# Macaron block: the mixer's three normalizations written by ScalarE instead of VectorE

## What is computed

```python
def _layernorm(x, axis=-1, eps=1e-05):
    m = jnp.mean(x, axis=axis, keepdims=True)
    v = jnp.var(x, axis=axis, keepdims=True)
    return (x - m) / jnp.sqrt(v + eps)

def _rmsnorm(x, w):
    v = jnp.mean(x * x, axis=-1, keepdims=True)
    return x * jax.lax.rsqrt(v + EPS) * w

# inside the mixer step, x is the layernorm of the stream
h = x + _mixer(_rmsnorm(x, norm1_w), in_proj_w, conv_w, conv_b, A_log, dt_bias, D, out_proj_w)
hn = _rmsnorm(h, norm2_w)
ffn = jax.nn.silu(hn @ gate_w.T) * (hn @ up_w.T) @ down_w.T
return h + ffn

# the whole
x = x + 0.5 * _L0_ffn_ref(_layernorm(x), ...)
x = x + _L0_attn_ref(_layernorm(x), ...)
x = x + 0.5 * _L0_ffn_ref(_layernorm(x), ...)
```

## Time and profile before

| what | us |
|---|---|
| median of 3 runs | 972.69 |
| lowest and highest of them | 969.92, 974.05 |
| the profiled execution | 979.37 |
| its span, first to last instruction | 977.6 |
| busy in the span: TensorE, its weight load | 718.4, 473.1 |
| busy: VectorE, ScalarE, GpSimd | 594.9, 364.3, 406.6 |
| VectorE on L1120, L959, L1195 in 300 to 700 us | 8.8, 7.8 (28 of 32), 7.0 |

### The profile page before, as it was taken

How to read it: one execution, slowest core, us unless ns; L and a number is a source line. 1 busy time by engine, 2 the same in 40 slices (tenths; PEclk the granted TensorE clock), 3 DMA queues, 4 the chain that set the end, 5 groups by cost and what they waited for, 6 DMA issues and landing times. The chain is left out here.

```text
span 977.6 us, 12866 instructions
## 1 busy us (share of the span) xinstructions
PE 718.4 (73%) x3584; PEld 473.1 (48%) x3584; DVE 594.9 (61%) x1898; ACT 364.3 (37%) x600; POOL 406.6 (42%) x540
## 2 busy tenths in 40 slices
PE   5777178887729689899998898686787537888860
PEld 3455157776503445353536354343454326777650
DVE  5744244454366888897887888873673333445427
ACT  2112033443308656656656565520111103344320
POOL 3755745554522333232332323210276562555550
PEclk9977579999959799999999999887788667999975
DMA  7311222222150000000000000000011122222208
GB/s 224 124 39 41 72 64 69 76 69 61 40 172 1 0 1 1 0 1 1 1 0 2 0 1 1 0 1 1 0 42 44 38 66 74 73 66 75 69 27 258
DMA packets 55892, 46.30 MB, mean 47 GB/s; under 512 B 8840, under 2 KB 51437, under 8 KB 55824
## 3 DMA queue, kind: packets, MB, share of 16 engines
q1 hardware_dynamic: 47120, 28.55, 10.7%
q0 software_dynamic: 8704, 16.93, 5.2%
HBM read 25.31 MB, written 21.19 MB: 48 GB/s over the span
## 5 line engine op out<-in xcount | busy, mean ns | idle before, releaser
L627 POOL DMA_INDIRECT ys<-arena,dest x144 | 140.8, 978 | 143.6 <-DVE arena L1444 89.3
L617 POOL DMA_INDIRECT xs<-rows,pos x128 | 124.3, 971 | 76.8 <-DVE pos L1364 39.0
L1820 PE MATMUL ps_go<-w_down_e,arena 128*128 x576 | 79.0, 281 | 8.7 <-DVE arena L1444 7.9
L1820 PEld LDWEIGHTS ps_go<-w_down_e,arena 128*128 128x128 f32 x576 | 71.5, 195 | 11.3 <-issue 11.3
L1434 DVE TENSOR_TENSOR hid<-silu_a,ps_b 128x512 f32<-128x512 f32 x36 | 24.7, 686 | 59.1 <-issue 36.2
L1783 PE MATMUL ps_tr<-ident,arena 128*128 128x128 f32 x144 | 29.9, 285 | 40.9 <-DMA arena<-xs 40.7
L1809 PE MATMUL ps_go<-ident,hid 128*128 128x128 f32 x288 | 44.8, 279 | 19.0 <-ACT arena L896 17.1
L1444 DVE COPY arena<-ps_go 128x256 f32<-128x256 f32 x72 | 30.5, 424 | 45.3 <-remote 28.2
L879 ACT ACTIVATE xt_hi<-ps_tr 128x256 fp32r<-128x256 f32 x72 | 27.6, 383 | 81.6 <-PE ps_tr L1783 73.3
L896 ACT ACTIVATE arena<-ps_go 128x512 f32<-128x512 f32 x72 | 43.0, 597 | 38.6 <-remote 31.2
L1537 PE MATMUL ps_a<-arena,w_tap 128*32 128x512 f32 (+1 forms) x120 | 56.0, 611 | 0.0
(11 more groups left out here) (275 smaller groups left out, 1843.7 us busy)
## 6 DMA issues: line engine op xcount, KB each, us to landing
arena<-xs SPq DMA_DIRECT2D x144, 65.0 KB
rows<-ys SPq DMA_DIRECT2D x8, 512.0 KB, 4.2
arena<-ys SPq DMA_DIRECT2D x8, 512.0 KB, 7.7
ys<-arena,dest POOLq DMA_INDIRECT x144
x<-in_L_attn_x SPq DMA_DIRECT2D x8, 256.0 KB, 6.4
arena<-in_L_ffn_ew SPq DMA_DIRECT2D x4, 512.0 KB, 7.1
xs<-rows,pos POOLq DMA_INDIRECT x128
out<-x SPq DMA_DIRECT2D x8, 256.0 KB, 3.6
```

Source lines behind the costliest of these rows:

```text
L617: pool.indirect_dma_start(xs, bass.IndirectOffsetOnAxis(pos[:, n, k * TT + t:k * TT + t + 1], 0), rows[:, n * TT + t, :], None).then_inc(s ...
L627: pool.indirect_dma_start(ys, bass.IndirectOffsetOnAxis(dest[:, i:i + 1], 0), y_out[:, p % YRING, j, :], None, bounds_check=2 * TOK - 1, o ...
L1820: r = pe.matmul(ps_k[:, j * P:(j + 1) * P], hid_t[:, p % 2, at:at + P], w_down_e[:, bass.ds(which[2 * p + j], 1), k, :].rearrange("p a d - ...
```

## The change

All three normalizations move to ScalarE, as activations with a factor column as scale and, for the first two, an offset column as bias: (x - mean) * r becomes x * r + (-mean * r). GpSimd makes the offsets, three small instructions more a block, and `azr` becomes two buffers deep, as is `offset`. The offsets stand before `arstd_ready` is raised. Two new waits in `pool_norms` guard the buffers against readers of two blocks earlier. In ScalarE's body `z_norm` stands ahead of `zt_copy`, `h_norm` ahead of `hnt_copy`, and `h_start` last. `enter` on VectorE loses its normalization between two `combine` steps.

```diff
-        azr = sb("azr", [P, TT])
+        azr = sb("azr", [P, 2, TT])
+        offset = sb("offset", [P, 2, 2, TT])
...
         def pool_norms(pool, b, q):
...
             pool.wait_ge(amv_ready, n + 1)
+            after(pool, zn_ready, n - 1)
+            after(pool, hb_ready, n - 1)
...
-            pool.tensor_tensor(azr[:, :], arstd[:, q, :], asmall[:, 0, :], ALU.mult).then_inc(arstd_ready, 1)
+            step(pool.tensor_tensor(azr[:, q, :], arstd[:, q, :], asmall[:, 0, :], ALU.mult))
+            step(pool.tensor_scalar(asmall[:, 1, :], amv[:, q, :, 0], -1.0, None, ALU.mult))
+            pool.tensor_tensor(offset[:, q, 0, :], asmall[:, 1, :], azr[:, q, :], ALU.mult)
+            pool.tensor_tensor(offset[:, q, 1, :], asmall[:, 1, :], arstd[:, q, :], ALU.mult).then_inc(arstd_ready, 1)
...
         def act_mixer(act):
+            def z_norm(b, q):
+                n = SQ * b + q
+                act.wait_ge(arstd_ready, n + 1)
+                after(act, zt_ps_ready, n)
+                for t in range(TT):
+                    r = act.activation(zn[:, t, :], x_tile(b, q, t), ACT.Identity, bias=offset[:, q, 0, t:t + 1],
+                                       scale=azr[:, q, t:t + 1])
+                r.then_inc(zn_ready, 1)
+            def h_start(b, q):
+                n = SQ * b + q
+                act.wait_ge(arstd_ready, n + 1)
+                after(act, hnt_ps_ready, n)
+                for t in range(TT):
+                    r = act.activation(hb[:, t, :], x_tile(b, q, t), ACT.Identity, bias=offset[:, q, 1, t:t + 1],
+                                       scale=arstd[:, q, t:t + 1])
+                r.then_inc(hb_ready, 1)
+            def h_norm(b, q):
+                n = SQ * b + q
+                act.wait_ge(hr_ready, n + 1)
+                for t in range(TT):
+                    r = act.activation(hb[:, t, :], hb[:, t, :], ACT.Copy, scale=hsm[:, 2, t:t + 1])
+                r.then_inc(hn_ready, 1)
...
                 if then:
+                    z_norm(*then)
                     zt_copy(*then)
...
                 if now:
+                    h_norm(*now)
                     hnt_copy(*now)
...
                     tm_copy(*next, 0)
+                    h_start(*next)
             def enter(n):
+                z_norm(*n)
                 zt_copy(*n)
...
-        def dve_mixer_norm(dve, b, q):
...
-            def h_start(b, q):
...
-            def h_norm(b, q):
...
             def enter(n):
...
                 combine(1)
-                combine(2)
-                dve_mixer_norm(dve, *n)
-                for m in range(3, NB):
+                for m in range(2, NB):
                     combine(m)
```

More of the change, by code:

```diff
@@ L486, in pool_norms @@
             n = SQ * b + q
-            own = Steps(pool, own_pool_pre, 6, n)
+            own = Steps(pool, own_pool_pre, 8, n)
             def step(instruction):
@@ L671, in act_mixer, with x_tile @@
             owns = [None]
+            def x_tile(b, q, t):
+                return x[:, (b * SQ + q) * TT + t, :]
+            def z_norm(b, q):
[20 more added lines that the diff above has]
+                r.then_inc(hn_ready, 1)
             def step(instruction):
@@ L1225, in body @@
                     outputs(*now, 0)
-                if then:
-                    dve_mixer_norm(dve, *then)
                 if now:
@@ L1252, in body @@
                     phase_sums(*next)
-                if now:
-                    h_norm(*now)
                 if next:
@@ L1275, in body @@
                     c_relative(*next)
-                    h_start(*next)
             def enter(n):
```

## The result

Run in turn, the changed kernel took 976.69 us (median of 20 runs, 970.43 to 983.66), the kernel before 971.01 (20 runs, 963.93 to 976.64). The ratio is 1.0068, with a 95% interval of 1.0046 to 1.009: the change made the kernel slower by 5.7 us, or 0.7%. The forecast was +7.9.

The account below looks back on a forecast made before the run. VectorE is busiest, but ScalarE, GpSimd and TensorE arrive just ahead, so relief is waited away. Entry 3.7, first pass 0.7, slow-clock passes 2 x 0.5, last two 1.4 and 0.4, clock 0.7: +7.9 on 972.7, 980.5 us; range 972 to 987.

Parts of the forecast that it names:

- What one group costs: Moved norms on ScalarE: 0.49 us per two-column instruction, 1.66 a group of four; `h_norm` 0.40 each, 1.3 a group.
- Rival A: ScalarE's second column is free and the groups are short: 4.6 us slower in all, 977 us; chance 0.22.
- GpSimd's part: The offset steps on GpSimd ahead of the norms add 0.76 us; the new buffer waits add nothing.
- A pass: Mixer pass with three blocks in flight: about 0 change for the fast kind, 0.5 us longer where TensorE was already later.
- (1): Pass head: `h_start` on ScalarE pushes `dt_parts` by 1.56 us, 0.62 absorbed by a gap, so `dt_sum` comes 0.94 later.
- (4): Pass end: `h_norm` adds 0.43 us, `hn_ready` is 0.54 later, and VectorE waits at `ffn_hidden(0)`, losing the 1.5 saved.
- Rival C: VectorE sets the pass, so passes give 1.5 us back: -3.5 us, or 957 us with the heads; chance 0.08.
- The entry: Mixer start, without cover: block 0 costs 1.3 us and block 1 2.4 us more, 3.7 in all, all kept.
- First full pass: Pass from 331 to 378 us: a ScalarE gap hides `h_start`; GpSimd's 0.76 and `h_norm` make it 0.7 us longer.
- the clock: TensorE's wait before `h_norm`'s transposes grows from 2.2 to about 2.6 us; half a pass more at lower clock, 0.7 us.
- rival B: TensorE's clock falls in all passes after the longer wait, three more at 1.34 us each: 984 us; chance 0.18.
- Pass without `then`: Pass 8, with no block to normalize at its head: `h_start` adds 0.94 us and `h_norm` 0.43, 1.4 in all.

Follow-up runs that it names:

- first pair: One profiled execution each of the kernel before and the changed kernel, all three norms on ScalarE; the mixer parts sum to 411.6 and 415.1 us.
- second pair: One more profiled execution each of the kernel before and the changed kernel, in a later session; the mixer took 408.0 and 417.6 us.
- second session: The unmodified changed kernel run again beside the kernel before; ratio 1.0093 (1.006 to 1.0126), +8.3 us.
- b_moved: Changed kernel with ScalarE's `h_start` moved ahead of `ffn_copy`, into the gap at the end of a pass; ratio to the kernel before 1.0045.
- a_znorm: Kernel before with only `z_norm` moved to ScalarE, plus GpSimd's offsets; ratio 1.0124, +12.0 us.
- a_pool: Kernel before with GpSimd making the offsets and holding `arstd_ready` for them, all three norms still on VectorE; ratio 1.0046, +3.7 us.

## Why the prediction was right, by its own steps

**What one group costs: right.** 478 to 482 ns against 0.49, groups of 1.63 to 1.65 us against 1.66, 387 ns against 0.40 for one column. From 298 ns without a column the first adds 89 and the second 91 to 95, where the forecast had 108 for one and 0.49 us for two together. Rival A, a second column that costs nothing, falls with this row.

**GpSimd's part: too small by 0.5 us.** `bc_norms` starts 1.11 us after L508 (480.49 to 481.60), where before it was 0.15 after L503: 0.96 more, against 0.76. This miss is L511's 0.38 us in place of 0.20. One of the seven instructions that were there before has grown too, and the sum had nothing for it:

```profile
478.77 0.52 POOL L506 TENSOR_SCALAR asmall<-asmall 128x4 f32<-128x4 f32 x1 [0.20 <-POOL asmall L504]
```

It took 0.23 us before. Counted from the start of the pass `bc_norms` ends at 12.79 us, where the forecast had 12.28 (481.72). So it is GpSimd that `bc_normed` waits for (0.20 us), and not ScalarE's chain, which the forecast put last by 0.3.

**A pass: right, to a tenth.** Counted from the start of the pass: (1) `dt_sum` at 8.04 instead of 7.24, 0.80 later (0.94 forecast). (2) `bc_normed` at 12.82 instead of 12.63, 0.19 later (forecast between -0.1 and 0). (3) its transposes on TensorE 14.54 instead of 14.35. (4) those of `h_norm` at 34.71 instead of 34.18, 0.53 later (forecast 0.54), and `ffn_hidden(0)` at 38.17 instead of 38.23, behind a wait of 1.10 (forecast about 1.3). The pass: 45.06 instead of 45.12, as forecast 0; and one with a clock fall 46.6 instead of 46.1, as forecast 0.5. Rival C, that VectorE sets the pass, is thereby out: it needed `h_norm` 1.3 us sooner.

**The entry: right in place, the size between the two traces for more than one reason.** ScalarE at block 1, after:

```profile
304.80 1.08 ACT L742 ACTIVATE zs<-ps_tr 128x512 f32<-128x512 f32 x2
305.75 1.65 ACT L689 ACTIVATE arena<-x,offset,azr 128x128 f32<-128x128 f32 x4
308.15 0.20 ACT L719 ACTIVATE arena<-arena 128x3 f32<-128x3 f32 x1 [0.75 <-PE ps_b L1532]
```

From the end of the silus (305.88) to L719 are 2.3 us, where before L683 followed at once; 2.4 was forecast. Block 0's part is less clean: its first projection started 1.5 us later (forecast 1.3), but the next one was 0.9 shorter than before in the first pair and 0.6 longer in the second, by the clock. So the whole entry came out 3.0 and 4.9 longer, with 3.7 forecast and 3.9 at an equal projection; that 3.7 lies between the two is in part luck. `zt_copy` of block 1, forecast near 311, came at 308.15; in this execution the mixer's statistics began 2.2 us earlier, so it answers to 310.35. What I had not seen is that TensorE's wait of 3.1 us for `z_norm` can be followed by a clock fall of its own.

**First full pass: two errors that cancelled.** TensorE ahead of `h_norm`'s transposes in this pass, before and then after:

```profile
366.43 1.12 PE L1525 MATMUL ps_tr<-ident,arena 128*128 128x128 f32 x4 [2.26 <-DVE arena L1195]
```

```profile
368.45 0.66 PE L1532 MATMUL ps_tr<-ident,arena 128*128 128x128 f32 x4 [2.56 <-ACT arena L706]
```

Counted from the pass's start (330.99 and 331.80) they are 1.2 us later, where I had 0.7; but before they ran at the lower clock (1.12) and after at the full one (0.66), which took 1.5 us from what follows, and the pass came out 0.3 shorter. In the second pair, with the full clock there in both, it came out 0.8 longer.

**The step that failed: the clock.** I took 0.7 us for more falls behind a longer wait, and gave 0.18 to rival B, in which every pass falls. The wait did grow, from 2.2 to 2.54 us. In the other five passes of the first pair the clock fell twice after and twice before. In the second pair it fell in one pass of these five before (46.0) and in two after (46.6, 46.7). So B falls, and of a growth with the wait nothing is shown either way. The last part is one more place: the output projection (L1644) took 1.98 us after and 3.29 before, and the part is 1.0 shorter instead of 0.4 longer; in the second pair, with 1.98 in both, it is 0.5 longer. The forecast of +7.9 lies between the two pairs of traces. It is 2.2 us above the difference of the medians in the result, and 0.4 below that of the second session (8.3).

**Pass without `then`: right in its first half, the total in part luck.** `dt_sum` waited 2.07 where it had waited 1.12, 0.95 more (0.94 forecast), and TensorE came to the output projection 0.88 later. That projection then took 1.98 us, where before it took 3.51, at the lower clock; other falls stand behind it, and the pass was 1.2 longer (1.4 forecast).

```profile
615.23 0.69 DVE L1038 TENSOR_TENSOR arena<-arena 128x512 f32<-128x512 f32 x1 [2.07 <-ACT arena L756]
```

## What to carry to other kernels

Before work is taken off the busiest engine, read from its rows who arrives just ahead of it: here ScalarE was 0.1 us and GpSimd 0.4 us from being late, and so 2.4 us of relief in a pass bought nothing, while the entry, which nothing covers, cost 3.0 to 4.9. What gained were a transfer into a gap that nobody waits behind, and an instruction put into a wait of its own engine. When a pass has two chains of nearly equal length, shortening one shows only the other, as the 1.39 to 0.51 and 0.20 to 0.95 of b_moved do.

## What the runs showed of the hardware

**GpSimd's small instructions stretch beside some of VectorE's.** A tensor_tensor on 128x4 takes 0.20 us. L511 took 0.38 in the pass shown above, and again 0.38 in all the full passes of the changed kernel but the first; in the first, and in most passes of a_znorm, it took 0.68 to 0.70. GpSimd in a_znorm, and VectorE at that time:

```profile
361.00 0.70 POOL L511 TENSOR_TENSOR offset<-asmall,arstd 128x4 f32<-128x4 f32 x1
```

```profile
360.95 0.69 DVE L1196 TENSOR_TENSOR zs<-zs,us 128x512 f32<-128x512 f32 x1
```

L511 ends at 361.70, just behind VectorE's instruction with two operands in SBUF (361.64). In the changed kernel it ends at 481.64, behind this one (481.57):

```profile
481.08 0.49 DVE L1172 SCALAR_TENSOR_TENSOR state<-state,decay,state_new 128x256 f32<-128x256 f32 x1
```

L506 shows the same. It took 0.52 us in the pass shown (478.77 to 479.29), beside `dt_sum` (478.51 to 479.20), and 0.23 in the passes of b_moved, where `dt_sum` was over before it began (358.70 and 359.23). And L511 took 0.20 in a_pool, where VectorE stood idle at that time.

The Trainium skill ("GPSIMD Engine Reference", section "Specifications") names contention on the SBUF interfaces with VectorE's instructions that have two inputs in SBUF. These rows agree; no run was made for it alone. A price read from one row of a small GpSimd instruction can be short by half a microsecond (0.20 against 0.70).

**A fall of TensorE's clock behind short waits.** It was seen behind waits of 0.76 and 0.98 us close together (3 times of 8), behind one of 2.2 to 2.6, and behind one of 3.14 (in one of four traces with this wait). Which of several equal waits is followed by 1.2 GHz could not be told from the rows, and it moves the sum of one execution by several us.

**A column on ScalarE costs about the same each time.** 298 ns without, 387 with one and 478 to 482 with two, on 128 elements.
